# AdaLN transformer block on one core: constants in one transfer, the front's work in another order, twenty-six leading matmuls

## The reference

```
mod = (silu(c) @ wmod).reshape(2, 6, 1, -1)        # sa, ca, ga, sb, cb, gb
ga, gb = sign * max(|.|, 0.25)                     # gates, at least 0.25 in size
h = layernorm(x) * (1 + ca) + sa
x = x + ga * (h @ blockmask(weight).T + bias)      # 32x32 blocks on where the mask has a nonzero sum
h = layernorm(x) * (1 + cb) + sb
x = x + gb * lora_ffn(h)      # silu(h1) * h3, then w2; each of w1, w3, w2 with a LoRA term
```

## Time and profile before

| | |
|---|---|
| median of 3 runs | 278.69 us |
| the profiled execution | 278.56 us, its span 277.0 us |
| busy: PE, PEld, DVE, ACT, POOL | 250.8, 197.7, 128.4, 87.0, 57.2 us |
| DMA | 24.06 MB, 87 GB/s over the span |
| chain of waits that ended last, by engine | PE 79%, DVE 8%, issue 4%, ACT 3%, DMA 3% |

### The profile page before, as it was taken

One profiled execution on the slowest core, in us unless ns is written; L12 is line 12 of the kernel. 1 busy time (PEld: TensorE's weight loads), 2 busy tenths in 40 slices (PEclk: granted clock), 3 DMA queues, 4 the chain that ended last, 5 costly groups with the idle time before them and its releaser, 6 DMA issues.

```text
span 277.0 us, 3318 instructions
## 1 busy us (share of the span) xinstructions
PE 250.8 (91%) x1196; PEld 197.7 (71%) x1196; DVE 128.4 (46%) x212; ACT 87.0 (31%) x144; POOL 57.2 (21%) x69
## 2 busy tenths in 40 slices
PE   6399759987949999999999999999999999999990
PEld 4277547665628888888888887888888888888770
DVE  0716812985992998546554742171110111200245
ACT  2225549108421434565462331111110101111100
POOL 1401626660640241320330100041000000000012
PEclk9999979999968999999999999999999999999997
DMA  6999910015022233132314540007400000000004
GB/s 188 394 380 407 395 76 0 5 17 190 6 79 69 76 114 117 52 99 80 111 38 116 88 26 0 2 2 39 151 0 0 1 0 2 0 0 0 2 0 153
DMA packets 12660, 24.06 MB, mean 87 GB/s; under 512 B 1250, under 2 KB 2786, under 8 KB 12644
## 3 DMA queue, kind: packets, MB, share of 16 engines
q1 hardware_dynamic: 12208, 23.65, 28.0%
q10 hardware_dynamic: 436, 0.20, 0.3%
HBM read 21.22 MB, written 2.10 MB: 84 GB/s over the span
## 4 chain that ended last, share of the span: by engine, by line
PE 79%; DVE 8%; issue 4%; ACT 3%; DMA 3%; POOL 1%; SPq 1%; DVEq 0%; ACTq 0%; POOLq 0%
PE up_a L1009 22%; PE up_b L1009 21%; PE acc L1022 7%; PE acc L1024 7%; PE acc L1023 7%; DMA wmod_sb<-in_wmod 3%; PE acc L960 2%; PE side L878 2%; PE acc L866 2%; DVE parts L697 2%; PE side L990 2%; DVE stats L626 1%; ACT hbuf L502 1%; PE up_b L890 1%; ACT ht_hi L493 1%
## 5 line engine op out<-in xcount | busy, mean ns | idle before, releaser
L812 DVE TENSOR_TENSOR g<-up_b,g 128x512 f32<-128x512 f32 (+1 forms) x22 | 15.2, 690 | 73.5 <-PE up_b L1009 73.5
L1022 PE MATMUL acc<-w_hi,g_hi 128*128 128x512 f32 (+1 forms) x88 | 34.8, 396 | 0.0
L1023 PE MATMUL acc<-w_lo,g_hi 128*128 128x512 f32 (+1 forms) x88 | 34.8, 395 | 0.0
L1024 PE MATMUL acc<-w_hi,g_lo 128*128 128x512 f32 (+1 forms) x88 | 34.8, 395 | 0.0
L721 DVE SCALAR_TENSOR_TENSOR raw<-side,raw 128x512 f32<-128x512 f32 (+2 forms) x33 | 21.4, 677 | 27.4 <-PE side L990 20.8
L601 ACT ACTIVATE g<-up_a 128x512 f32<-128x512 f32 (+1 forms) x22 | 13.1, 598 | 62.0 <-PE up_a L1009 62.0
L606 ACT ACTIVATE g_hi<-g 128x512 fp32r<-128x512 f32 (+1 forms) x22 | 13.9, 632 | 52.9 <-DVE g L812 52.9
L399 POOL TENSOR_TENSOR xt<-work,xt 128x512 f32<-128x512 f32 x5 | 6.8, 1378 | 113.0 <-DVE work L736 113.0
L524 ACT ACTIVATE w_hi<-raw 128x512 fp32r<-128x512 f32 (+2 forms) x33 | 20.3, 626 | 28.6 <-DVE raw L721 28.6
L1009 PE MATMUL up_a<-ht_hi,w_hi 128*128 128x512 f32 (+1 forms) x88 | 25.4, 412 | 0.6 <-ACT w_hi L524 0.6
L1009 PE MATMUL up_a<-ht_hi,w_lo 128*128 128x512 f32 (+1 forms) x88 | 24.9, 406 | 0.0
(11 more groups left out here) (149 smaller groups left out, 347.0 us busy)
## 6 DMA issues: line engine op xcount, KB each, us to landing
raw<-in_ffn SPq DMA_DIRECT2D x33, 256.0 KB, 2.6
wmod_sb<-in_wmod SPq DMA_DIRECT2D x4, 1024.0 KB, 11.2
xt<-in_x SPq DMA_DIRECT2D x8, 256.0 KB, 8.2
wmod_sb<-in_wmod SPq DMA_DIRECT2D x1, 2048.0 KB, 15.6
out<-xt SPq DMA_DIRECT2D x8, 256.0 KB, 2.9
mask_sb<-in_mask SPq DMA_DIRECT2D x4, 256.0 KB, 10.6
wa<-in_weight SPq DMA_DIRECT2D x4, 256.0 KB, 10.7
lora_raw<-in_lora SPq DMA_DIRECT2D x2, 320.0 KB, 7.3
```

Of the source, the lines that this page charges most:

```text
L812: nc.vector.tensor_tensor(g[0:w], up_b[0:w], g[0:w], ALU.mult).then_inc(g_ready, 1)
L1022: nc.tensor.matmul(acc[t][:], hi, down_hi[j][0:w], start=(j == 0), stop=False)
L1023: nc.tensor.matmul(acc[t][:], hi, down_lo[j][0:w], start=False, stop=False)
L1024: last = nc.tensor.matmul(acc[t][:], lo, down_hi[j][0:w], start=False, stop=(j == HT - 1))
```

## The change

`ident` (the identity), `c` and the constants become one array `const` of 268 columns in one DMA; `silu_c` is cleared by GpSimd and only its used columns are written. ScalarE's bias split moves behind `norm(3)`. VectorE takes the first moments ahead of the constants. `WARM_MATMULS` goes from 10 to 26; `fill(6)` between the modulation's first half and the transposes goes, the others become 3, 3, 2 for 2, 4, 3. `masked_weight_low` moves from VectorE to GpSimd. The gates of batch 0 and their spread move ahead of batch 1's transposes, and the banks of these change. `add_x1(2)` goes to GpSimd and `spread(0)` behind the roots of pass 2, whose norms VectorE and ScalarE share. `lora_part` of the two late pieces moves behind step 0's `g_lo`. SP's queue: LoRA piece 0 ahead of the gate's 1 MB.

```diff
-WARM_MATMULS = 10
+WARM_MATMULS = 26
-X1_POOL = (0, 1, 4, 5, 6, 7)
+X1_POOL = (0, 1, 2, 4, 5, 6, 7)
-FILL_MOD, FILL_TURN, FILL_COLS, FILL_H = 6, 2, 4, 3
+FILL_TURN, FILL_COLS, FILL_H = 3, 3, 2
@@ turn_bank
-            return (acc[k], (acc[1], acc[2], acc[3], acc[1])[k], (up_b, up_a, *side)[k])[i]
+            return (acc[k], (acc[1], acc[0], acc[2], acc[3])[k], (up_b, up_a, *side)[k])[i]
@@ sync
             load_x(1)
+            load_lora(0)
             load_mod(GATE_A, SHIFT_F, wmod_ga_loaded)
-            load_lora(0)
@@ gpsimd
             root(0, 2)
+            root(2, 2)
...
+            masked_weight_low(0)
             low(0)
+            masked_weight_low(1)
             low(1)
+            masked_weight_low(2)
             low(2)
-            low(3)
             root(T, 2)
             root(T + 2, 2)
+            masked_weight_low(3)
+            low(3)
...
-            spread(0)
             add_x1(0)
             add_x1(1)
+            add_x1(2)
             root(2 * T, 2)
             root(2 * T + 2, 2)
+            spread(0)
             spread(1)
@@ scalar
             norm(2)
             norm(3)
+            bias_high()
...
             whole(3)
+            gate_size(0)
             norm(T + 2)
             norm(T + 3)
+            gate_copy(0)
+            gate_copy(1)
             high(4)
...
             mod_evacuate(1)
             gate_size(1)
+            norm(2 * T)
+            norm(2 * T + 1)
             weight_high(0)
@@ vector
-            dve.wait_ge(const_loaded, 16)
-            nc.vector.tensor_copy(half_on[:], const[:, HALF_ON:HALF_ON + 2]).then_inc(half_on_ready, 1)
             moment(0)
             moment(1)
             moment(2)
             moment(3)
+            dve.wait_ge(const_loaded, 16)
+            nc.vector.tensor_copy(half_on[:], const[:, HALF_ON:HALF_ON + 2]).then_inc(half_on_ready, 1)
...
             mask_weight(3)
+            gates_of(0)
             moment(4)
...
-            add_x1(2)
             add_x1(3)
             moment(2 * T)
             moment(2 * T + 1)
+            moment(2 * T + 3)
+            moment(2 * T + 2)
+            centres(2 * T)
+            norm(2 * T + 2)
+            norm(2 * T + 3)
             columns(1)
-            moment(2 * T + 2)
-            moment(2 * T + 3)
             gates_of(1)
-            lora_part(2)
-            for n in range(2 * T, 3 * T):
-                norm(n)
             merge(0)
             merge(1)
             weight_low(0)
             weight_low(1)
+            lora_part(2)
...
-                if s == 0:
-                    for n in range(LORA_EARLY, len(LORA_CUTS)):
-                        lora_part(n)
                 if more:
                     merge(3 * (s + 1))
...
                                         ALU.subtract).then_inc(g_low_ready, 1)
+                if s == 0:
+                    for n in range(LORA_EARLY, len(LORA_CUTS)):
+                        lora_part(n)
@@ tensor
             mod_rows_part(0, (0, 1))
-            pe.wait_ge(ident_loaded, 16)
-            fill(FILL_MOD)
...
-            for m in range(3):
-                attend(0, 2, m)
+            attend(0, 2, 0)
+            gate_rows(0)
+            attend(0, 2, 1)
+            attend(0, 2, 2)
+            attend(0, 3, 0)
+            gate_spread(0)
+            gate_spread(1)
             turn(4)
             turn(5)
-            gate_rows(0)
-            attend(0, 3, 0)
             turn(6)
-            gate_spread(0)
             turn(7)
-            gate_spread(1)
...
-            for m in range(3):
-                attend(1, 1, m)
+            attend(1, 1, 0)
             columns(1)
+            attend(1, 1, 1)
+            attend(1, 1, 2)
```

More of the change, by code:

```diff
@@ L53 @@
 HALF_ON = P + 2
-CONST_COLS = P + 4
+IDENT = P + 4
+MOD_C = IDENT + P
+CONST_COLS = MOD_C + B * KT
 PASSES = [(0, 0), (1, 0), (0, 1), (1, 1)]
@@ L86, with build @@
 SIDE = {job: n for n, job in enumerate(SIDE_JOBS)}
-def build(nc, x, mask, weight, bias, ffn, lora, c, wmod, identity, consts, out):
+def build(nc, x, mask, weight, bias, ffn, lora, wmod, consts, out):
     x_rows = x.rearrange("(b p t) d -> b p t d", b=B, p=P)
@@ L118, in build @@
         exponent = sb("exponent", [P, T])
-        centre = sb("centre", [P, 2 * T])
+        centre = sb("centre", [P, 3 * T])
         half_on = sb("half_on", [P, 2])
@@ L399, in add_x2, with masked_weight_low @@
                 nc.gpsimd.tensor_tensor(xt[:, b, t], work[:, t], xt[:, b, t], ALU.add).then_inc(x2_by_pool, 1)
+            def masked_weight_low(k):
+                pool.wait_ge(wa_high_ready, k + 1)
+                nc.gpsimd.tensor_tensor(wa_lo[k][:], wa[:, k], f32(wa_hi[k][:]), ALU.subtract).then_inc(wa_ready, 1)
             pool.wait_ge(ones_ready, 1)
@@ L456, in _, with bias_high @@
                 act.dma_start(bias_raw[row * QUAD:row * QUAD + 1], bias[row:row + 1]).then_inc(bias_loaded, 16)
[L457 to L463, removed]
+            act.wait_ge(const_loaded, 16)
+            act.wait_ge(silu_c_cleared, 1)
+            nc.scalar.activation(silu_c[:, :, 0:B], const[:, MOD_C:MOD_C + B * KT].rearrange("p (k b) -> p k b", b=B),
+                                 ACT.Silu).then_inc(silu_c_ready, 1)
+            def bias_high():
+                act.wait_ge(bias_loaded, 32)
+                act.wait_ge(bias_cleared, 1)
+                for row in range(2):
+                    at = slice(row * QUAD, row * QUAD + 1)
+                    nc.scalar.activation(bias_parts[at], bias_raw[at], ACT.Copy).then_inc(bias_high_ready, 1)
             def mod_evacuate(second):
@@ L471, in norm @@
                 i, t = divmod(n, T)
-                act.wait_ge(centre_ready, n - T * i - 1 + 2 * i)
+                act.wait_ge(centre_ready, 2 * i + 2)
                 if i:
-                    act.wait_ge(turned, KT)
-                nc.scalar.activation(work[:, t], xt[:, i, t], ACT.Identity, bias=centre[:, n:n + 1],
+                    act.wait_ge(turned, KT * i)
+                nc.scalar.activation(work[:, t], xt[:, PASSES[i][0], t], ACT.Identity, bias=centre[:, n:n + 1],
                                      scale=rstd[:, n:n + 1]).then_inc(normed_by_act, 1)
@@ L622, in moment @@
                     dve.wait_ge(x_loaded[b][t], 16)
[L623 to L628, removed]
+                at = moment_place(n)
+                if at >= 2:
+                    dve.wait_ge(moments_ready, at - 1)
+                nc.vector.bn_stats(stats[:, at % 2], xt[:, b, t]).then_inc(stats_ready, 1)
+                dve.wait_ge(stats_ready, at + 1)
+                nc.vector.bn_aggr(moments[:, n], stats[:, at % 2]).then_inc(moments_ready, 1)
             def norm(n):
@@ L865, in turn @@
                 for t in range(T):
-                    last = nc.tensor.transpose(dst[:, t * P:(t + 1) * P], work[:, t, k * P:(k + 1) * P], ident[:])
+                    last = nc.tensor.transpose(dst[:, t * P:(t + 1) * P], work[:, t, k * P:(k + 1) * P], ident)
                 last.then_inc(turned, 1)
@@ L870, in turn_tile @@
                 dst = free_side(("turn", t))
-                pe.wait_ge(normed, 2 + T + t + 1)
+                pe.wait_ge(normed, 6 + t + 1)
                 for k in range(KT):
-                    last = nc.tensor.transpose(dst[:, k * P:(k + 1) * P], work[:, t, k * P:(k + 1) * P], ident[:])
+                    last = nc.tensor.transpose(dst[:, k * P:(k + 1) * P], work[:, t, k * P:(k + 1) * P], ident)
                 last.then_inc(turned, 1)
@@ L898, in columns @@
                     at = second * HALF + c * P
-                    last = nc.tensor.transpose(up_a[:, at:at + P], mod_rows[:, second, c * P:(c + 1) * P], ident[:])
+                    last = nc.tensor.transpose(up_a[:, at:at + P], mod_rows[:, second, c * P:(c + 1) * P], ident)
                 last.then_inc(cols_out, 1)
@@ L1150, in launch_inputs @@
         consts[:, HALF_ON + n] = p // RANKS == n
+    consts[:, IDENT:IDENT + P] = np.eye(P)
+    consts[:, MOD_C:] = by_feature(c.T).reshape(P, KT * B)
     return {
```

40 lines of the change are left out of this document (14 added, 26 removed).

## The result

The changed kernel takes 271.11 us (median of four runs, 269.73 to 272.08) against 278.83 us: ratio 0.9723, 95% interval 0.9664 to 0.9781. Run again beside other kernels it had 271.8 us, ratio 0.9735 (0.9697 to 0.9773). The forecast was 268.4 us, range 265.6 to 272.4: right way, inside the stated range but above the forecast case's own (266.4 to 270.2), the gain of 7.7 us three quarters of the 10.3 that it stood for. The profiled execution took 272.02 us, span 270.4.

The account below looks back on a forecast made before the run. TensorE was taken to bound the feed-forward from `merge(6)` on, so gains come only from its earlier gaps. Steps of 4.0 + 1.05 + 0.7 + 4.45 give 10.2 us off 278.56: 268.4 us, range 265.6 to 272.4.

Parts of the forecast that it names:

- forecast case: Whole kernel: the main outcome, 268.4 us with its own range 266.4 to 270.2; chance 0.60.
- cases 1 to 3: The rivals of leading matmuls, GpSimd bound and late gate load: 271.9, 270.4 and 269.4 us; chances 0.12, 0.16, 0.05.
- Checkpoint 1: Front up to `columns(0)`, before at 21.03 us: lead 4.0 us, between 0.5 and 4.4.
- rival 1: Front: the leading matmuls don't bring the clock up, lead there 0.5 us, time 271.9 us; chance 0.12.
- Checkpoint 2: Up to `attend_bias(1)`, before at 47.80 us: lead 5.05 us, the 4.93 us gap becoming about 2.75.
- wait of 3.45 us: After batch 1's transposes and `attend_last(0)`: TensorE waits 3.45 us for ScalarE's eight `high`/`whole` steps.
- 0.3 or 0.8 us: Subtractions on GpSimd blocking VectorE's masking steps: 0.8 us charged; by a bandwidth split some 0.3 us.
- Checkpoint 3: Up to `merge(2)`, before at 68.94 us: lead 5.75 us, with a new 2 us wait at `merge(0)`.
- Checkpoint 4: Feed-forward's first steps up to `merge(6)`, before at 88.78 us: lead 10.2 us, this step 4.45, bounds 3.5 to 5.2.
- rival 2: Front: GpSimd becomes the bound through blocks of whole instructions, +2 us, time 270.4 us; chance 0.16.
- rival 3: Gate's load is late, its cover gone by 1 us more, time 269.4 us; chance 0.05.
- rival 4: New gaps hold TensorE's clock at 0.50 from 35.6 us to `merge(2)`, adding 16 us, 284.4 us; chance 0.04.

Follow-up runs that it names:

- experiment 1: The changed kernel run again with no edit: 271.8 us, ratio 0.9735 to the kernel before.
- Experiment 3: Changed kernel with ten leading matmuls in place of 26, nothing else: 273.0 us, ratio 0.9791 to the kernel before.
- experiment 12: experiment 11's kernel with the four masked-weight subtractions on VectorE, the fourth behind the centres: 265.52 us, ratio 0.9533 to the kernel before.
- experiment 5: Changed kernel with GpSimd's `masked_weight_low(3)` and `low(3)` ahead of batch 1's two roots instead of behind: 270.9 us, ratio 0.9707 to the kernel before.
- experiment 9: Changed kernel with one added wait: GpSimd's `masked_weight_low(3)` starts only after VectorE's two centre steps of batch 1: 270.05 us, ratio 0.9684 to the kernel before.
- experiment 8: Changed kernel with 18 unread matmuls added before batch 1's transposes and 9 before `merge(0)`: 271.98 us, ratio 0.9744 to the kernel before.
- experiment 4: Changed kernel with the four masked-weight subtractions back on VectorE in their old places: 270.39 us, ratio 0.9695 to the kernel before.
- experiment 7: Changed kernel with GpSimd's `spread(0)` moved back from behind pass 2's roots to ahead of the adds: 268.71 us, ratio 0.9636 to the kernel before.
- Experiment 2: Changed kernel with VectorE's two late lora pieces back ahead of step 0's merges: 276.29 us, ratio 0.9882 to the kernel before.
- experiment 10: Changed kernel with batch 1's moments ahead of the gates and `spread(0)` ahead of the adds: 266.33 us, ratio 0.9557 to the kernel before.
- experiment 6: Changed kernel with VectorE taking batch 1's four moments ahead of `gates_of(0)`: 267.22 us, ratio 0.959 to the kernel before.
- experiment 11: experiment 10's kernel with GpSimd's wait for the centres added: 265.31 us, ratio 0.9537 to the kernel before.

## Why the prediction was right, and where its sizes were off

The direction and the way there were right: a lead in the first 17 us, a second one behind the feed-forward's first step. In between the prediction was wrong, by its own signs as well: it called itself wrong if `up(1,0)` came later than 74 us (it came at 74.91) or if the clock was 0.50 anywhere between 45 and 80 us (it was, twice). By checkpoint it had gains of 4.0, 1.05, 0.7 and 4.45 us; they came as 4.46, -0.89, -1.50 and 3.91. The two in the middle are 4.1 us short. The median is only 2.7 us above the forecast, since the feed-forward behind `merge(6)` was 0.6 us shorter than before and the profiled execution 0.9 us above the median. That the number is inside the stated range is in part luck: the range reached up to 272.4 for cases 1 to 3, while about half of the 4.2 us missing came from three falls of the clock (0.35, 1.3 and 0.5 us, below), which none of these cases had.

**Checkpoint 1**, forecast 4.0 us, measured 4.46. Each part came as early as forecast or earlier: 26 matmuls end at 9.3, the transposes start at 11.95, `columns(0)` runs at 16.57. VectorE's moments started at 4.73 and ended at 8.55, x's last tile having landed 0.8 us earlier than before. But 0.86 us of the lead is the first weights, which let TensorE start at 10.23 where it was 11.09 before and 11.0 in the forecast; in experiment 1, at 10.81, the lead is 3.86. Since this start differs by 1 us between executions, that part is luck. Experiment 3 shows that the leading matmuls did bring the clock up; rival 1 falls.

**Checkpoint 2**, forecast lead 5.05, measured 3.57: the first step that failed. The gap of 2.75 us came as 4.37. I had the four moments' end at 32.65 (measured 32.6) and then "root 1.1, centre", which left out that `masked_weight_low(3)`, which the change puts right behind the roots, would hold a centre step of 0.16 us for 1.0 us more. I had charged the move of the subtraction with 0.8 us at the masking steps; they took 0.92, 1.27 and 1.62 us where 0.69 is the length unheld, 1.7 us too long together, of which the profile of experiment 12 puts 0.4 us on the path. I had not looked at the small steps at all. Experiments 5 and 9 show the block as it moves and as it goes: 1.0 of the 1.5 us. Another 0.35 us is the transposes at half clock, by experiment 8. The wait of 3.45 us before `attend_bias(1)` that I had named came as 0.82, because TensorE was late itself: from its transposes to the end of `attend_last(0)` it took 6.5 us where I had 3.65.
The Trainium skill, "SBUF — State Buffer", section "SBUF: two separate sides", has it that of two such instructions the one that starts first holds the shared port pair for its whole length. The traces agree: 1.14 us against 0.16, and the end of the held small step lies within 0.15 us of the end of the holder in the changed kernel and in experiments 4 and 5. What I had weighed as 0.3 or 0.8 us was about 1.4 on the path, 1.0 at the centre and 0.4 at the masking steps by the profile of experiment 12.

**Checkpoint 3**, forecast lead 5.75, measured 2.07: the larger failure, 2.2 us by itself. The new wait for `spread(0)` was forecast at 2 us and is 2.31. That experiment 7 gains 2.8 us by undoing it shows that it was a loss, where I had entered it as a shift. Its second half was missed: the clock falls on it, `merge(0)` and the attention block behind it take about 1.3 us longer, and the transposes wait for TensorE and no longer for the norms. The other 0.9 us are the later spread, 0.5, and the stretch from the transposes to `merge(2)`, 5.57 us for 5.2.

**Checkpoint 4**, forecast 4.45, measured 3.91 (5.98 less 2.07). Up to `up(1,0)` it came as written, 4.12 us for 4.15: the gap of 4.77 us became 0.18 and 0.85, plus 0.41 for `weight_low`, and the moved lora pieces took 2.17 us behind GpSimd's adds where they had taken 4.20 beside them. The clock fell all the same near 77 us, and step 1 took 7.9 us for 6.7 and a wait of 0.7. Without that fall, in experiment 1, the same stretch takes 7.39 us with a wait of 0.93, so the term was right and the fall cost 0.5. Experiment 2 measures the edit at 4.1 us.

**Rivals.** 2 (GpSimd as the bound of the front) was right in its cause, but what counted was 1.0 us at one small step, where it had 2 us at the masking steps. 3 fell: the gate's rows ran at 26.70, uninterrupted. 4, the slower one, has its mechanism in the trace, three falls of the clock, but each ends after 3 to 7 us.

## What to carry to other kernels

Before moving work to GpSimd, list VectorE's instructions with two SBUF inputs that can start while it runs, the tiny ones first: a step of 0.16 us on the path waited for the end of a neighbour of 1.25 us, and one wait on the other engine bought 1.0 us back. An engine that waits in its list for a late input should first do what is ready (moments ahead of gates, 4 us; lora pieces behind the merges, 4 us). A lead won at the front is worth only what the later gaps let through. Filling or removing a gap that another engine bounds isn't a gain in itself: in experiments 8 and 10 the fall of the clock came at the next gap instead.

## What the runs showed of the hardware that was not expected

The clock fell to 0.50 after a gap of 2.31 us that came behind 10 us of unbroken work, and near 77 us after gaps of only 0.85 and 0.41 us, where in the other profiled execution of the same kernel (experiment 1) it held. The same gap of 3.15 us before `attend_bias(1)` passed without a fall in experiments 6 and 12 (1.16 us for its four matmuls) and brought one in 10 and 11 (2.04 us). No run here shows what decides it.

The modulation's first weights let TensorE start between 10.16 and 11.16 us in executions of kernels with the same queue of transfers, and what follows moves with it: in experiment 7, at 11.06, `attend_bias(1)` is 0.88 us later than in the changed kernel.
